# Subtracting the last row of each expert's W1 on GpSimd, before and between its first scatters, and not on VectorE

## What is computed

```python
x = x + cross_attention(layernorm(x), ctx)          # scores, softmax, values, Wo
xt = layernorm(x)
p = softmax(xt @ Wr + br); probs, idx = top_k(p, 2); probs /= probs.sum()
h = einsum('td,edf->etf', xt, W1) + b1              # W1: 8 x 128 x 512
h = layernorm(relu(h), g1, be1)
y = einsum('etf,efd->etd', h, W2) + b2              # W2: 8 x 512 x 128
y = layernorm(relu(y), g2, be2)
x = x + sum over the token's two experts of probs * y
```

## Time and profile before

| what | value |
|---|---|
| time, median of 3 runs | 329.19 us (328.3, 329.19, 329.69) |
| span of the profiled execution | 268.4 us |
| median less span | 60.8 us |
| profiled execution's own time | not listed apart from its span |
| VectorE busy | 229.7 us, 86% |
| ScalarE busy | 211.5 us, 79% |
| GpSimd busy | 190.6 us, 71% |
| TensorE busy | 239.9 us, 89% |

### The profile page before, as it was taken

One profiled execution on the slowest core, in us unless ns is written; L12 is line 12 of the kernel. 1 busy time (PEld: TensorE's weight loads), 2 busy tenths in 40 slices (PEclk: granted clock), 3 DMA queues, 4 the chain that ended last, 5 costly groups with the idle time before them and its releaser, 6 DMA issues.

```text
span 268.4 us, 10286 instructions
## 1 busy us (share of the span) xinstructions
PE 239.9 (89%) x2960; PEld 194.0 (72%) x2960; DVE 229.7 (86%) x1091; ACT 211.5 (79%) x795; POOL 190.6 (71%) x300
## 2 busy tenths in 40 slices
PE   1989779899888677679899999999999999999994
PEld 1564567777666434579899979999999999999330
DVE  0667986867689989689999988999999999999875
ACT  2465675789888888757999988999999999999700
POOL 8602277877757777775888888888888888878640
PEclk9997995899999759999999999999999999999999
DMA  6998398123425234354333443333315686772257
GB/s 159 313 299 295 91 271 279 51 89 92 139 82 136 83 91 99 84 119 94 84 90 67 89 82 81 73 72 75 84 33 142 155 155 141 149 143 86 68 187 233
DMA packets 48676, 34.56 MB, mean 129 GB/s; under 512 B 26871, under 2 KB 42743, under 8 KB 48620
## 3 DMA queue, kind: packets, MB, share of 16 engines
q1 hardware_dynamic: 38972, 22.80, 32.8%
q0 software_dynamic: 6592, 9.00, 12.7%
q10 hardware_dynamic: 3056, 2.11, 2.6%
HBM read 15.11 MB, written 12.02 MB: 101 GB/s over the span
## 4 chain that ended last, share of the span: by engine, by line
DVE 37%; issue 22%; PE 20%; ACT 9%; DMA 5%; DVEq 4%; SPq 1%; ACTq 0%
PE bank L721 15%; DVE vo L1873 8%; PE bank L725 4%; DMA w2f<-in_L_ffn_W 3%; DVE rs L1914 3%; DVE cx L1903 3%; DVE kq L1866 3%; DVE w2f L1653 3%; DVEq L1880 2%; DVE st L1891 2%; ACT ex L1175 2%; DVE mv L1897 1%; DMA wr<-in_L_ffn_Wr 1%; ACT xt L1198 1%; DVE topi L1573 1%
## 5 line engine op out<-in xcount | busy, mean ns | idle before, releaser
L679 POOL DMA_INDIRECT answers<-vo,words_of x71 | 70.6, 994 | 23.8 <-issue 19.4
L667 POOL DMA_INDIRECT slot_rows<-pay,pos x64 | 65.5, 1023 | 27.9 <-issue 18.5
L721 PE MATMUL bank<-kb_room,w1h 128*128 128x128 f16 x568 | 55.2, 219 | 1.7 <-issue 1.7
L725 PE MATMUL bank<-w2h,rh 128*128 x284 | 51.4, 219 | 1.6 <-ACT w2l L1122 1.6
L725 PE MATMUL bank<-rh 128*128 128x129 f16 x284 | 51.5, 220 | 0.0
L725 PE MATMUL bank<-w2l,rh 128*128 x284 | 51.4, 219 | 0.0
L721 PE MATMUL bank<-kb_room,w1l 128*128 128x128 f16 x284 | 51.2, 219 | 0.0
L1866 DVE SCALAR_TENSOR_TENSOR kq<-bank,rh 128x512 f16<-128x512 f32 x71 | 47.8, 673 | 0.1
L721 PEld LDWEIGHTS bank<-kb_room,w1h 128*128 x568 | 43.6, 98 | 2.6 <-issue 2.6
L1347 ACT ACTIVATE rh<-bank 128x512 f16<-128x512 f32 x71 | 41.1, 579 | 5.2 <-PE bank L721 4.2
L705 POOL DMA_DIRECT2D words_of<-slot_rows x71 | 40.8, 576 | 2.0 <-issue 1.8
(11 more groups left out here) (259 smaller groups left out, 601.7 us busy)
## 6 DMA issues: line engine op xcount, KB each, us to landing
x_tok<-in_x SPq DMA_DIRECT2D x8, 256.0 KB, 7.7
w1f<-in_L_ffn_W SPq DMA_DIRECT2D x2, 1024.0 KB, 8.8
pay<-pay SPq DMA_DIRECT2D x8, 256.0 KB, 3.3
w1f<-answers SPq DMA_DIRECT2D x8, 256.0 KB
w2f<-answers SPq DMA_DIRECT2D x8, 256.0 KB, 2.9
kb_room<-slot_rows SPq DMA_TRANSPOSE x71, 3.3
words_of<-slot_rows POOLq DMA_DIRECT2D x71, 1.0 KB
answers<-vo,words_of POOLq DMA_INDIRECT x71
```

Of the source, the lines that this page charges most:

```text
L667: eng.indirect_dma_start(slot_words, bass.IndirectOffsetOnAxis(ap=pos[:, g % 2, k, i:i + 1], axis=0), pay[g % 2][:, k, i, :].bitcast(U32), ...
L679: eng.indirect_dma_start(answers, bass.IndirectOffsetOnAxis(ap=words_of[:, j % NW, 0:1], axis=0), z[j % NZ], None).then_inc(s_ans[j % NZ], 16)
L721: return eng.matmul(dst, lhsT, rhs, start=start, stop=stop)
L725: return eng.matmul(dst, lhsT, rhs, start=start, stop=False, skip_group_check=True)
```

## The change

The table `LESS_LAST` and VectorE's function go. GpSimd gets the same function, with the same operands. It does experts 0 and 1 between its two sets of selects, experts 2 to 5 behind the second set, expert 6 behind the first four scatters of group 0 and expert 7 behind the next four.

```diff
-        LESS_LAST = {2: {2: (0,), 16: (1,), 17: (2,), 21: (3,)}, 3: {3: (4,), 5: (5,), 7: (6,), 9: (7,)}}
...
+            def less_last(e_):
+
+                if e_ % H == 0:
+                    eng.wait_ge(ld_w1[e_ // H], 16 * (1 + H))
+                eng.tensor_tensor(cols(w1f, e_)[0:D - 1, :], cols(w1f, e_)[0:D - 1, :], w1_last[e_][0:D - 1, :],
+                                  ALU.subtract).then_inc(s_w1x, 1)
+
             for n in range(2):
+                if n == 1:
+                    less_last(0)
+                    less_last(1)
                 c, first = (FIRST, 0) if n == 0 else (TILES - FIRST, FIRST)
                 from_act(eng, f"key_bias{n}")
...
                 t.then_inc(s_sel, 1)
+            for e_ in range(2, E - 2):
+                less_last(e_)
...
                     for i in range(GT):
                         if g < GROUPS - 1 or k == 0:
                             payload_out(g, k, i)
+                    if g == 0:
+                        less_last(E - 2 + k)
...
             def weights(n, place):
-                for e_ in LESS_LAST.get(n, {}).get(place, ()):
-                    w_less_last(e_)
                 for c in CENTRE.get(n, {}).get(place, ()):
```

More of the change, by code:

```diff
@@ L1637, in weight_scale @@
                                              op1=ALU.mult).then_inc(s_scale, 1)
[L1639 to L1643, removed]
             def w_centred(n):
```

## The result

The changed kernel takes **338.57 us** (median of 4 runs, 338.13 to 338.77) against 328.75 us for the kernel before on the same chip (median of 4 runs, 328.09 to 329.69): ratio **1.0277**, 95% interval 1.0218 to 1.0336. That is +9.8 us, where the prediction had +2.5 us and a range up to 333.8 us. It is slower, as forecast, by four times as much. The ratios in this text are taken over a kernel's fast runs, those within about 1.5% of its lowest, so a ratio can differ from the quotient of the medians.

What follows compares the result with a forecast made beforehand. It took the chain from VectorE's group 0 payload subtraction through the W2 load to ScalarE as the bound in the changed stretch. Terms +3.4 and -0.9 gave +2.5 us, so 331.7 us; forecast 330.8 to 332.8, range 327.9 to 333.8.

Steps and rivals of the forecast that it cites:

- Bounds of the stage: Between 20 and 51 us the chain decides: VectorE's delays before 31.3 us have no cover, those from 32 to 44 do.
- What is removed, -0.9: Eight subtractions leave VectorE; group 2's steps shorten by 1.9 us, of which 0.9 us reaches the time.
- One subtraction, 1.2 us: Length of one 127x512 two-input subtraction on GpSimd, with ends of 0.60 and 2.0 us.
- The turn-taking: Behind the selects VectorE gets one two-input operation in per GpSimd subtraction of experts 2 to 5: +3.4 us.
- upper end of +6.5: VectorE's delay behind the selects if one GpSimd subtraction takes 2.0 us.
- Keeps its 1.8 us of cover: At ScalarE's squares of W2, group 1's VectorE and TensorE work moves equally with W2, staying 1.8 us ahead.
- Experts 0 and 1 at nothing: Two subtractions before the key-bias selects cost 0, covered by GpSimd's 11 us idle or VectorE's 1.28 us wait.
- Experts 6 and 7 at nothing: Subtractions between group 0's scatters cost 0; expert 6 can hold VectorE 1.2 us, under the W2 wait.
- GpSimd's lateness: GpSimd starts group 4's scatters 1.2 us late, covered by 2.54 us of idle time before the first answer.
- 60.8 us around the span: Median 329.19 less the 268.4 us span leaves 60.8 us outside it, taken as unchanged.

Runs made afterwards that it cites:

- e9: The change, unedited, on a 270 chip beside the kernel before: 278.66 us, ratio 1.0326.
- e8: The kernel before, unedited, on a 270 chip, for a trace beside the change: 273.75 us, ratio 1.0131.
- e13: The change, unedited, on a 325 chip beside the kernel before: 333.24 us against 325.52, ratio 1.0126.
- e12: The kernel before, unedited, on a 325 chip, for a trace beside the change: 325.33 us, ratio 0.9987.
- e1: The kernel before with VectorE's eight subtractions cut to one column of 512: 271.41 us, ratio 1.0007.
- e11: The change with each GpSimd subtraction replaced by a one-input multiplication by 1.0: 273.69 us, ratio 1.0158.
- e4: The change with each GpSimd subtraction split into four of 128 columns: 335.37 us, ratio 1.0342.
- e7: The change, unedited, on a 325 chip: 333.33 us against 325.77 for the kernel before, ratio 1.0233.
- e5: The change with a one-column memset behind each GpSimd subtraction of experts 2 to 5: 332.37 us, ratio 1.0212.
- e2: The change with experts 2 to 4 behind group 0's first four scatters, 5 to 7 behind the next four: 274.43 us, ratio 1.0141.
- e3: The change with experts 2 to 5 back on VectorE in turn 2 of its group loop: 270.67 us, ratio 1.0015.
- e10: The change with experts 2 to 4 and 5 to 7 behind group 0's scatters, repeated on another 270 chip: 275.63 us, ratio 1.012.
- e0: The kernel before, unedited, profiled on another 270 chip: 272.26 us, ratio 0.9992.
- e6: The change with experts 2 to 5 on VectorE, 0 with 6 and 1 with 7 behind group 0's scatters: 326.53 us, ratio 1.0034.

## Why the size was wrong

- **Bounds of the stage: right.** The payload subtraction of group 0 had no cover, and what held it decided the case. On one chip the payload moved by 5.0 us and the span by 5.4 (e9, e8), on another by 5.7 and 6.1 (e13, e12).
- **What is removed, -0.9: not visible.** VectorE's part is the 1.9 us that was read; on the time e1 shows 1.0007.
- **One subtraction, 1.2 us: right,** 1.23 us from start to start. The Trainium skill (GPSIMD Engine Reference, section Performance versus the Vector engine) led to an estimate of 1.12 us; the measured 1.23 is above it.
- **The turn-taking: the step that failed.** "A VectorE operation that reads two tensors of SBUF gets in once between two GpSimd instructions that read SBUF" came from the 0.24 us period beside the selects. It holds for one-input instructions of GpSimd (e11: at most 1.17 us), and for the two-input quarters in front of the selects (e4). For the four subtractions right behind the selects, which the prediction priced with it, it fails in every trace (the change's first profile, e7, e9, e13, and e4 and e5 with their edits): one two-input operation of VectorE waits out all four, from up to 0.9 us before the first of them. The prediction let VectorE come as far as the probabilities and then wait, +3.4 us. In the repeats it stopped at the logits, before MAX8, the one-hots, the mask and the probabilities, and did all of those afterwards: +5.0 to +5.7. Its upper end of +6.5 had held this size for the wrong reason (2.0 us a subtraction).
- The Trainium skill (SBUF — State Buffer, section Who interferes with whom) says that the instruction which starts later "fully blocks". The traces agree with the block and go beyond it: by that rule, as the prediction took it, an operation waits for one instruction of 1.23 us, and it waited for four; why it got its turns in other places, no run shows.
- **"Keeps its 1.8 us of cover": wrong, through TensorE.** The prediction moved all of group 1 by one amount. TensorE's idle time of 5.7 us for the mask came before 6 us more at 0.50, and its work came later than W2 (e9; on a 325 chip e12 shows ScalarE not waiting for W2 even before the change, at 47.29, so nothing can be read there).
- **Experts 0 and 1 at nothing: right in some executions only.** The prediction let them delay the selects by 1 us at most, under VectorE's wait of 1.28 us, and left out that they hold VectorE. In e2, e3 and e9 they held later operations or none (1.20 and 0.86 us in e2, 0.85 in e9), and e2's payload is at 31.44, as in the kernel before (31.20 to 31.89). In the change's first profile (22.57 and 23.87) and in e10 they held two operations of the later 24 tiles' statistics, for 2.1 and 2.2 us more than these take elsewhere; the payload was later by 1.9 us of its 7.4 and by 1.6 us. Part of that can be the execution's own, since these operations began later too, before any hold (22.57 against 21.37 in the kernel before).
- **Experts 6 and 7 at nothing: half right.** Expert 6 held VectorE 1.99 us, not 1.2, and once W2 was no longer last that stood on the chain (45.12 in the change's first profile, 43.62 in e9); in e3, where W2 was still last (squares at 48.65 after 1.51 us of waiting), it cost nothing.
- **GpSimd's lateness: no cost seen,** as said. Group 4's scatters follow without a gap in e9 (0.30 us, where e8 has 2.15), and before the first answer GpSimd was idle 2.18 us for ScalarE.
- **60.8 us around the span: wrong.** It set a trace of a 270 chip against times of a 325 chip.

**What is left of the size.** +5.4 and +6.1 us between two traces of a pair, +7.6 to +9.8 between medians. Part of the rest goes with the granted clock, which the prediction left out. All profiled executions on 270 chips, with the clock of the stretch 24 to 108 us of each (at least two chips stand in this table; that of the first profile is not on record):

| kernel | clock in 24 to 108 | payload at | first expert products | span |
|---|---|---|---|---|
| before, first profile | 0.87 | 31.20 | 108.56 | 268.4 |
| before, e0 | 0.83 | 31.29 | 110.76 | 270.6 |
| before, e8 | 0.80 | 31.89 | 112.06 | 272.2 |
| e11, one input | 0.88 | 34.78 | 110.80 | 270.6 |
| e3, four on VectorE | 0.86 | 36.12 | 112.69 | 272.2 |
| before with one column, e1 | 0.82 | 31.94 | 112.03 | 272.0 |
| behind scatters, e2 | 0.88 | 31.44 | 110.55 | 270.3 |
| behind scatters, e10 | 0.81 | 33.45 | 116.84 | 276.6 |
| change, e9 | 0.78 | 36.91 | 116.13 | 277.6 |

The kernel before alone spans 3.8 us between 0.87 and 0.80. At like clock a payload later by 4.9 us costs 3.8 (e3 against the first profile; e3's late payload, from key biases at 30.00, is this execution's own, which took 273.84 us against its median of 270.67), one later by 3.6 us costs 2.2 (e11). The payload is not all of it: e10, whose longest holds come after it, is 4.4 us over e8 at a like clock with a payload 1.6 us later. From the experts' first products to the end all but e9 need 159.5 to 160.1 us (e9 161.5): the time is settled by then. The change is late and had a low clock as well; all its four runs on that chip were at 278 or more, where before has some at 269. That its hole on TensorE brings the low clock on is what e9's stretches suggest, and on 325 chips it is so in most: 0.67 (its first profile), 0.68 (e13) and 0.76 (e7) with the change, 0.72 (e4) and 0.68 (e5) with its edited forms, against 0.76 in e12 and 0.81 in e6, which have no such hold before the payload. No run shows the clock apart from the hold.

**What stays open.** What the waits are that cost some 54 us on 325 chips; how much of the loss beyond 6 us is the change's own clock and how much the lot of the draw; and why VectorE gets its turns among two-input subtractions in front of the selects (between experts 0 and 1 in the change's first profile and in e10, after each quarter in e4), once among the quarters of expert 6, and never in the rows of two to four behind the selects or the scatters.

## What to carry to other kernels

Before work with two SBUF inputs goes from VectorE to GpSimd, count how many such instructions stand in a row there, and charge VectorE's next two-input operation with the whole row, from nearly a microsecond before the row's first record; a turn for each instruction came in some places only, so it is the better case and not the one to plan with. Cutting them up or putting memsets between did not help behind the selects; a place where VectorE has cover did, and so did a one-input form. Price a contention from a row of the same kind in the same place: what one-input selects do says nothing of a two-input subtraction. And compare a trace's span with its own run's time before adding one to the other: the sum of a span from one chip and a median from another is no baseline.

## What was not expected of the hardware

- Two-input GpSimd instructions in a row behind other GpSimd work shut out VectorE's two-input operations as one block: 5.84 us for four of 1.23, 3.48 and 3.70 for three, 2.63 for two, 7.26 for sixteen quarters. In the same place one-input ones (1.46 us each, 5.84 in all) let them in, with records up to 1.17 us. In front of the selects two-input ones let them in too, one for each quarter of 0.42 us in e4.
- A hold can begin up to 0.9 us before GpSimd's record of the instruction that causes it (27.33 against 28.21 in e9), and for expert 6 while the record of a scatter still ran.
- The same program takes 270 to 274 us on some chips and 325 to 329 us on others; in the one pair of traces of the kernel before (e8, e12), waits of up to 8.2 us on ScalarE that none of the core's own engines ends add up to 53.6 us, about the difference of 53.4.
